# State scan of a Mamba layer on one NeuronCore: a second buffer for the rectified step sizes, block 1's parts at step 3, and step 60's product with C on VectorE

## The reference, cut to what matters

```
D_MODEL, D_STATE, EXPAND = 512, 16, 2                 # D_INNER = 1024
x_dbl = x_conv @ W_x.T
delta, Bm, Cm = split(x_dbl, [D_INNER, D_INNER + D_STATE])
delta = softplus(delta @ W_dt.T + b_dt)
A = -exp(A_log)
for each time step t (512 of them):
    decay = exp(d_t[..., None] * A)
    state = decay * state + B_t[:, None, :] * x_t[..., None]
    y_t   = einsum('bds,bs->bd', state, C_t) + x_t * D
y = y * silu(z);  out = y @ W_out.T
```

## Time and profile before

| quantity | value |
|---|---|
| median of three runs | 2645.19 us |
| profiled execution | 2638.76 us |
| its span | 2637.0 us |
| TensorE busy | 2479.6 us (94% of the span) |
| VectorE busy | 1802.1 us (68%) |
| ScalarE busy | 1115.6 us (42%) |
| GpSimd busy | 592.7 us (22%) |
| first scan of the state scan starts at | 498.07 us |
| last product with C ends at | 724.79 us |

### The profile page before, as it was taken

How to read it: one execution, slowest core, us unless ns; L and a number is a source line. 1 busy time by engine, 2 the same in 40 slices (tenths; PEclk the granted TensorE clock), 3 DMA queues, 4 the chain that set the end, 5 groups by cost and what they waited for, 6 DMA issues and landing times.

```text
span 2637.0 us, 33262 instructions
## 1 busy us (share of the span) xinstructions
PE 2479.6 (94%) x11618; PEld 1682.7 (64%) x11618; DVE 1802.1 (68%) x1885; ACT 1115.6 (42%) x1366; POOL 592.7 (22%) x404
## 2 busy tenths in 40 slices
PE   6999989988776999999999999999898999999998
PEld 5778877654334777777655555554586777777775
DVE  5878854499978677778866666565444766666655
ACT  2334422466344222222245555554233455455543
POOL 4555544488842211111100000000000000000000
PEclk9999999999877999999999999999798999999999
DMA  7667755622021334344233222332112265666653
GB/s 273 234 239 263 265 162 176 248 72 72 0 97 48 128 155 164 127 165 154 97 120 114 96 96 73 107 110 72 64 65 118 106 227 218 225 239 223 222 215 138
DMA packets 124238, 394.73 MB, mean 150 GB/s; under 512 B 23729, under 2 KB 39293, under 8 KB 97137
## 3 DMA queue, kind: packets, MB, share of 16 engines
q1 hardware_dynamic: 95584, 326.82, 34.5%
q10 hardware_dynamic: 28560, 66.66, 7.1%
HBM read 304.14 MB, written 89.30 MB: 149 GB/s over the span
## 4 chain that ended last, share of the span: by engine, by line
PE 79%; DVE 8%; DMA 5%; issue 3%; POOL 3%; ACT 2%; ACTq 0%; SPq 0%; DVEq 0%; POOLq 0%
PE ps L2113 18%; PE ps L2114 17%; PE ps L2115 17%; PE ps L2500 10%; PE ps L2512 9%; PE ps L2407 3%; DMA w_halves<-unit_lo 3%; DVE ps L1646 2%; POOL work L955 2%; PE ps L2766 1%; DMA x_res<-in_x 1%; POOL work L936 1%; DVE ln_st L1516 1%; DMA wT_lo<-w_halves 1%; DVE work L1646 0%
## 5 line engine op out<-in xcount | busy, mean ns | idle before, releaser
L1866 DVE TENSOR_TENSOR sums<-sums,pT 128x1024 f32<-128x1024 f32 x272 | 313.7, 1220 | 188.1 <-ACT pT L1345 187.0
L1804 DVE SCALAR_TENSOR_TENSOR peak<-ps,rs_all,peak 128x1024 f32<-128x1024 f32 x272 | 335.7, 1278 | 93.9 <-PE ps L2407 93.7
L1345 ACT ACTIVATE pT<-ps,rs_all 128x1024 f32<-128x1024 f32 x272 | 278.4, 1130 | 226.4 <-PE ps L2500 224.3
L2512 PE MATMUL ps<-pT,values 128*64 128x512 f32 x1088 | 242.5, 596 | 0.0
L2512 PEld LDWEIGHTS ps<-pT,values 128*64 128x64 f32 x1088 | 74.5, 137 | 146.5 <-issue 133.8
L2230 PE MATMUL ps<-work,ident 128*128 128x512 f32 x256 | 130.3, 640 | 35.8 <-POOL work L936 18.8
L1005 POOL TENSOR_TENSOR cT_lo<-cT_raw,cT_hi 128x512 fp32r<-128x512 f32 x60 | 77.7, 1295 | 352.0 <-ACT cT_hi L1294 352.0
L2000 DVE TENSOR_TENSOR rgu_lo<-rgu_raw,rgu_hi 128x2048 fp32r<-128x2048 f32 x64 | 143.9, 2288 | 5.1 <-ACT rgu_hi L1428 5.0
L898 POOL TENSOR_TENSOR ctx_lo<-ctx_raw,ctx_hi 128x512 fp32r<-128x512 f32 x64 | 105.6, 1650 | 128.9 <-DVE ctx_hi L1551 128.9
L1646 DVE TENSOR_TENSOR_SCAN ps<-ps,work 128x1024 f32<-128x1024 f32 x50 | 114.3, 2286 | 15.2 <-ACT ps L1217 13.2
L2500 PE MATMUL ps<-q_lo,key_hi 64*128 64x512 f32 x544 | 120.6, 439 | 0.9 <-DMA scale_rows<-sd_rows_dram 0.7
(11 more groups left out here) (470 smaller groups left out, 6376.3 us busy)
## 6 DMA issues: line engine op xcount, KB each, us to landing
rgu_raw<-in_r_gate_up SPq DMA_DIRECT2D x64, 1024.0 KB, 4.8
rd_raw<-in_r_down SPq DMA_DIRECT2D x32, 1024.0 KB, 4.9
sh_raw<-in_s_parts SPq DMA_DIRECT2D x32, 768.0 KB, 4.3
key_rows<-key_hi SPq DMA_DIRECT2D x17, 1024.0 KB, 3.9
key_rows<-key_lo SPq DMA_DIRECT2D x17, 1024.0 KB, 5.9
value_rows<-values SPq DMA_DIRECT2D x17, 1024.0 KB, 8.9
ctxT_raw<-in_ctx_T SPq DMA_DIRECT2D x16, 1024.0 KB, 6.7
ctx_raw<-in_ctx SPq DMA_DIRECT2D x16, 1024.0 KB, 8.2
```

Source lines behind the costliest of these rows:

```text
L1345: nc.scalar.activation(pT[:, i], ps[:, b:b + 2], ACT.Exp, scale=rs_all[:, bass.ds(c * KT + attend_tile(j, i)[1], 1)]).then_inc(s4_exp.sem, 1)
L1804: nc.vector.scalar_tensor_tensor(peak[:, p], ps[:, b:b + 2], rs_all[:, bass.ds(c * KT + kt, 1)], peak[:, p], ALU.mult, ALU.max).then_inc(s ...
L1866: nc.vector.tensor_tensor(sums[:, p], sums[:, p], pT[:, i], ALU.add).then_inc(s4_sum.sem, 1)
L2512: done = nc.tensor.matmul(ps[e * DK:(e + 1) * DK, 6 + p], values[:, s, kt, h * DK:(h + 1) * DK], pT[:, i, e], start=start and kt == 0, sto ...
```

## The change

Three edits in the state scan. The rectified step sizes of odd blocks go to a new tile `relu_odd`, those of even blocks stay in `bc_rows`, and ScalarE waits for the addition of block k - 2 instead of k - 1 (for block 1 for none). `PARTS_STEP` of block 1 goes from 1 to 3, and with it its logarithm from step 2 to 4 and its addition from step 5 to 7. Step 60 leaves `FAR_STEPS`, so that VectorE does its product with C; two instead of three blocks of the projection's fourth row tile stand behind the accumulation of step 62.

```diff
-FAR_STEPS = (3, 8, 13, 18, 23, 28, 33, 37, 41, 45, 49, 53, 57, 60)
+FAR_STEPS = (3, 8, 13, 18, 23, 28, 33, 37, 41, 45, 49, 53, 57)
...
-PARTS_STEP = {1: 1, 2: 5, **{k: 11 + 4 * (k - 3) for k in range(3, IB)}}
+PARTS_STEP = {1: 3, 2: 5, **{k: 11 + 4 * (k - 3) for k in range(3, IB)}}
 LOG_STEP = {k: n + 1 for k, n in PARTS_STEP.items()}
 ADD_STEP = {k: n + 4 for k, n in PARTS_STEP.items()}
...
+        relu_odd = s2("relu_odd", [P, T])
...
+        def relu_rows(k):
+            return relu_odd if k % 2 else bc_rows
...
-                nc.gpsimd.tensor_tensor(delta[:, k, 1:T], bc_rows[:, 1:T], delta[:, k, 1:T], ALU.add).then_inc(dt_ready, 1)
+                nc.gpsimd.tensor_tensor(delta[:, k, 1:T], relu_rows(k)[:, 1:T], delta[:, k, 1:T], ALU.add).then_inc(dt_ready, 1)
...
                 if k:
-                    act_e.wait_ge(dt_ready, k)
-                    nc.scalar.activation(bc_rows[:, 1:T], ps[:, bank, 1:T], ACT.Relu, bias=b_dt[:, k:k + 1]).then_inc(dt_relu, 1)
+                    if k >= 2:
+                        act_e.wait_ge(dt_ready, k - 1)
+                    nc.scalar.activation(relu_rows(k)[:, 1:T], ps[:, bank, 1:T], ACT.Relu, bias=b_dt[:, k:k + 1]).then_inc(dt_relu, 1)
...
                 if n == STEPS - 2:
                     pe.wait_ge(sc_read, near_steps(n))
-                    for ib in range(3):
+                    for ib in range(2):
                         project_rows(ib, TT - 1)
-            for ib in range(3, IB - 1):
+            for ib in range(2, IB - 1):
                 project_rows(ib, TT - 1)
```

## The result

The changed kernel took 2630.3 us (median of 16 runs, 2621.43 to 2642.61) against 2642.97 us for the kernel before (16 runs, 2630.06 to 2650.75); these medians lie 12.7 us apart. The ratio of the two kernels' times, taken over all runs, is 0.996 with a 95% interval of 0.9943 to 0.9976: 0.4% or 10.6 us less, within 0.24% to 0.57%. Forecast were 2633 us, within 2624 to 2643, and a gain of 11.3 us. A second series of the changed kernel gave 0.9976 (0.9962 to 0.999, 12 runs), which is 6.3 us less; the two intervals overlap, and both leave out no change. The profiled execution took 2630.27 us, 8.5 us less than that of before.

The account below looks back on a forecast made before the run. VectorE was taken to bound the scan, so gains come from where it stands still: 8.1 us (opening, second buffer, block 6) plus 3.2 at the end make 11.3. Forecast 2633 us, range 2624 to 2643.

Parts of the forecast that it names:

- opening, to scan 9: Steps 0 to 8: block 1's parts later and no buffer wait cut VectorE's loss from 6.9 to 3.5 us, gain 3.4.
- second buffer, scans 9 to 17: Steps 15 and 16: relu of block 4 no longer waits; 2.8 and 1.1 us go, 0.4 comes back, gain 3.5.
- block 6 at step 24, to scan 25: Step 24: relu's wait of 1.02 us goes, block 6's product from TensorE takes its place with 0.4 left, gain 1.0.
- the end: Step 60: VectorE takes the product (+1.27 us), TensorE starts accumulation 60 earlier and ends at 727.9 instead of 731.0, gain 3.2.
- Pauses forecast at 0.6, 1.3 and 1.1: Scans 4, 5 and 6: losses left by the moved logarithm, block 2's late product from TensorE, and block 2's logarithm.
- the gates of blocks 0 and 1: Behind scans 8 and 16: gates wait 0.5 and 0.4 us for TensorE's accumulations of steps 7 and 15.
- The rule on the clock: TensorE: throttled state is the default, sustained activity releases it; accumulation 60 would take 1.73 us, no change to the sum.
- The rival that TensorE falls to the low clock in the scan and takes the lead: Seven places in the scan at 1.2 GHz, 12.3 us; with the slow tail 9 us slower, 2653 us; chance 4%.
- its second rival: Only the buffer counts: GpSimd or TensorE takes over in the opening, the move gives nothing, 3.4 us lost, 2636; chance 15%.
- The 1.9 us that the forecast read at step 1: Scan 1 started at 503.46 but could at 501.55, with block 1's softplus parts ahead of its decays; counted as VectorE's loss.

Follow-up runs that it names:

- step 60 only: Kernel before with only step 60's product moved to VectorE and two projection blocks instead of three behind step 62: device time 0.9993 of before, stretch 228.37 us.
- parts only: Kernel before with only block 1's parts moved to step 3 (logarithm 4, addition 7), one buffer, step 60 on GpSimd: device time 1.0014, stretch 236.54 us.

## Why the prediction was right, point by point

| step of the forecast | forecast | measured |
|---|---|---|
| opening, to scan 9 | 3.4 | 3.87 |
| second buffer, scans 9 to 17 | 3.5 | 3.50 |
| block 6 at step 24, to scan 25 | 1.0 | 0.25 |
| the end | 3.2 | 2.91 |
| sum | 11.3 | 10.53 |

The forecast's terms add to 11.1; it took 8.1 us for the first three, which it called the sum of the exact times, and so came to 11.3. The direction, the places and the sum held. Pauses forecast at 0.6, 1.3 and 1.1 (steps 4 to 6, by start times) were 0.4, 1.0 and 1.1, and the gates of blocks 0 and 1, forecast to wait 0.5 and 0.4, waited 0.40 and 0.35. The opening got 0.5 us more than forecast, most of it because accumulation 0 stood 0.5 us closer to scan 0 in this execution.

Step 24 was mis-sized: its scan's wait fell from 1.32 to 0.58, where the forecast left 0.4, and the gate of block 2 right behind it now waits 0.41 for TensorE, which the forecast did not follow up. The end was mis-sized by 0.3: an accumulation that waits for its input takes 1.98 to 2.0 us from its start, not the 1.73 of one in a queue, and only the last one counted.

The rule on the clock held at the end: accumulation 60 at 1.98 us instead of 3.48, with no change to the sum, as VectorE's read 63 was the bound. The rival that TensorE falls to the low clock in the scan and takes the lead is seen in small at one place, the gate of block 4, with 1.3 to 2.8 us in seven of 13 profiles and not 12; it was there without the quicker scan as well.

One thing was right in its number and wrong in its reading. The forecast booked 3.4 us of the opening to both edits, and its second rival said that without the move they would be lost. They are the buffer's but for some 0.5 us. The move of block 1's parts takes away the pauses of steps 1 and 2, and TensorE takes most of that back by the gate of block 0; without the second buffer the move costs 1.8 us. That rival was right about the engine, TensorE, and about the edit that gives next to nothing; only the 3.4 us were not lost with it.

And part of the nearness is luck. The 1.9 us that the forecast read at step 1 were 1.7 us of a slow clock in that one execution. By "step 60 only" the old opening reaches scan 9 at 35.30; the changed one, at 25.07 us behind an accumulation 0 that stood at 8.0 us on average over the eleven profiles with 12 products ahead, reaches it at 33.1. So the opening is worth some 2.2 us rather than 3.87, an estimate. The changed kernel's own stretch was 222.45 us in one execution and 227.27 in the other, and its gain in device time 10.6 and 6.3 us: a forecast of 11.3 lies at the upper end of what the runs bear out.

## What to carry to other kernels

Two edits at one place are worth what the next bound leaves, not the sum of the pauses they remove; measure each alone, since one of them may do nothing or harm. When a queue stands idle for one late item, look first for work of its own that can be issued ahead of it: TensorE's projection one step earlier did the same as taking the product off GpSimd, without adding to the saturated engine. Before a pause in a profile is counted as the kernel's, look at it in a second execution: one of 1.8 us here came from a slow clock that 13 other profiles don't have. Where a few us are at stake, compare stretches inside the profile and take out what differs between executions of one kernel, here 1.8 us by a transfer's landing and the clock of the matmuls behind it, and up to 2.8 by the clock at one gate.

## What the runs showed of the hardware that was not expected

The same pause of 2.8 us of TensorE, at the same place of the program, was followed by full clock in six profiles and by 1.2 GHz in seven, and within one kernel by either: the granted clock of the 3 us behind it was 1.00 in one execution of the changed kernel and 0.50 in the other (3.70 and 6.69 us for the same two accumulations). The pause of 2.63 us ahead of accumulation 33 was followed by the low clock in 11 of 14 profiles (7.11 us for three accumulations, at full clock 5.42); in the three where it was not, the clock was lost at accumulation 37. Pauses of 3.76, 4.07 and 4.38 us ahead of accumulation 0 were followed by the low clock (3.78, 3.64 and 3.78 us for one accumulation), those of 0.7 to 1.3 us in the stretch never; but one of 3.03 us (parts only, ahead of accumulation 5) was followed by full clock, 1.98 us for the accumulation. The length of the pause alone does not decide. The Trainium skill, TensorE: Matmul & The Clock Gate (Part 1, What's actually happening), says that the window in which the chip looks at activity runs free of the kernel, so that the number of slow matmuls varies from run to run of the same kernel. The two executions of the changed kernel agree with it; no run here shows that this is the cause.
